# Waits between GpSimd's row gathers in a graph network kernel

## The chip, the cores and the metric

The kernel runs on one core of a Trainium2 chip. The core has five engines that run their own instruction streams and meet only at semaphores: TensorE (PE, matrix products), VectorE (DVE), ScalarE (ACT), GpSimd (POOL) and SyncE (SP, which here only issues transfers). Data is moved between memory (HBM) and the on-chip buffer (SBUF) by 16 DMA engines, on which transfers are queued by SP, ACT or GpSimd. A transfer raises its semaphore by 16 when it has landed. The metric is the device time of one execution in microseconds, the median of three runs.

## The reference

3125 nodes with 256 features each are passed through two layers. Each layer adds to x the output of a graph stage, a mixer, and a mixture of experts. Only the two graph stages gather rows by edge, over 53125 edges sorted by destination:

```python
# layer 0: attention over edges, 4 heads of 64
e = leaky_relu(el[src] + er[dst], 0.2)
ex = exp(e - segment_max(e, dst)[dst])
alpha = ex / segment_sum(ex, dst)[dst]
rst = segment_sum(feat_src[src] * alpha[:, :, None], dst)
# layer 1: weighted sum over edges
support = xn @ weight
agg = segment_sum(support[src] * edge_weight[:, None], dst)
```

The second graph stage is computed as segment_sum(xn[src] * edge_weight) followed by the product with weight, so its gathers fetch rows of 256 numbers.

## The kernel before

The edges are cut into 416 chunks of 128 (NC). A chunk whose destinations cross a border between tiles of 128 nodes is worked on once for each tile, which makes 440 steps (NS). There are 25 tiles of nodes (T).

**The gathers.** One gather is one indirect DMA that GpSimd issues: it fetches 128 rows of a table in HBM, one row to each SBUF partition, at the row numbers that stand in a column of an index tile. `gather_rows` (L483 to L488) fetches rows of `feat_d`, 260 numbers each, into the tile `ring`, which has 24 places (RING) of four steps; step n goes to place n // 4 modulo 24, and the four gathers of a place raise one semaphore, `gathered[place]`. `fetch_rows` (L1205) fetches rows of a table of 256 numbers into the tile `rows`, which has 48 places (RING1) of one chunk, each with a semaphore of its own.

**Where they stand.** The stages run one behind the other, with a barrier of all engines between two. 440 gathers into `ring` are spread over three of them: gathers 0 to 31 in `node_projections`, 32 to 73 in `mixer_and_targets` (L721), and 74 to 439 in `first_aggregate` (L973). In the last, before each fourth gather, GpSimd waits (`once(pool, summed, ...)`) until TensorE has used the place that is to be overwritten, so it can be 96 steps ahead of TensorE at most. 416 gathers into `rows` follow much later: 0 to 19 (PREFILL) in `second_mixer` (L2053), and 20 to 415 in `second_aggregate` (L1264 to L1278). There, before each fourth gather, GpSimd waits until TensorE has finished all but 20 of the steps of that number; it also computes 13 small roots (L1267) in between.

**Who reads them.** In the first aggregation VectorE and ScalarE wait for a whole block of 32 steps before the last four groups of the block ahead, scale the rows (L1086, L1116), and TensorE multiplies them with a one-hot matrix (L1187); VectorE adds the product to its tile (L1071). In the second, TensorE's step n waits for gather n, for VectorE's one-hot matrix (L1286) and for the addition three steps back, multiplies (L1378), and VectorE adds (L1295). Of each 32 steps some also carry a piece of the mixer's attention and of a two-layer network for a pair of tiles (L1385 to L1417).

Nothing in GpSimd's stream waits for a gather to land: the only waits between gathers are those for a free place. The order of the work is written out by hand in each engine's function, without a scheduler.

Of the kernel before, what the change touches and what calls it, by code (L numbers as in the profile page):

```python
# [51 lines left out]
RING = 24  # L52
# [7 lines left out]
AHEAD = 2 * R  # L60
UP_FIRST = 2 * MAXB // UP
RING1 = 48
PREFILL = 20
CLEAR_AT = 18
PARTY = [4, 4, 4, 4, 4, 5]
PARTY_END = [sum(PARTY[:n + 1]) for n in range(len(PARTY))]
assert sum(PARTY) == T
assert NC == CB * SB and NC - RING1 * (NC // RING1) > 0 and RING1 >= T - 1 + 8
assert T % R == 0 and NS == RB * SB and NS % MAXB == 24 and RB <= P
# [67 lines left out]
def once(eng, sem, n, hold=None):  # L137

    if isinstance(n, int) and n <= 0:
        return  # L140
    if hold is None:
        eng.wait_ge(sem, n)
    else:
        hold(eng, sem, n)
# [46 lines left out]
def program(nc, A, out):  # L191
    with ExitStack() as top:
# [69 lines left out]
        with kept:  # L262
# [19 lines left out]
            with Stage(nc) as held:  # L282
                rows = sb("rows", [P, RING1, D], ctx=held)
                step_slot = sb("step_slot", [1, NS], I32, ctx=held)
# [199 lines left out]
def gather_rows(pool, ring, gathered, src_lane, table, n):  # L484

    q, at = divmod(n, 4)
    pool.indirect_dma_start(ring[:, q % RING, at, :], None, table,  # L487
                            bass.IndirectOffsetOnAxis(ap=src_lane[:, n:n + 1], axis=0)).then_inc(gathered[q % RING], 16)  # L488


def node_projections(nc, A, hold, bank, const, big_k, big_v, scores, dst_lane, src_lane, xn_d, xnT_d, feat_d, ring,
                     gathered, end_row, decay, link):

# [192 lines left out]
def mixer_and_targets(nc, A, bank, const, k1, v1, fold, scores, part_er, er, step_tile, src_lane, dst_lo_d, feat_d, ring,  # L686
# [4 lines left out]
    with Stage(nc) as ctx:  # L691
# [27 lines left out]
        @block.gpsimd  # L719
        def _(pool):  # L720
            for n in range(EARLY[NI + 1], BY_THEN):  # L721
                gather_rows(pool, ring, gathered, src_lane, feat_d, n)

        @block.vector
# [140 lines left out]
def first_aggregate(nc, bank, const, acc, er, part_er, dst_lo_d, step_tile, src_lane, dst_lane, feat_d, ring, gathered, masks, decay, link, fold,  # L865
# [10 lines left out]
    with Stage(nc) as ctx:  # L876
# [94 lines left out]
        @block.gpsimd  # L971
        def _(pool):
            for n in range(BY_THEN, NS):  # L973
                if n % Q == 0:
                    once(pool, summed, n - RING * Q + Q)
                gather_rows(pool, ring, gathered, src_lane, feat_d, n)

        @block.vector
# [226 lines left out]
def fetch_rows(pool, rows, gathered, src_of, table, n):  # L1205

    pool.indirect_dma_start(rows[:, n % RING1, :], None, table,  # L1207
                            bass.IndirectOffsetOnAxis(ap=src_of[:, n:n + 1], axis=0)).then_inc(gathered[n % RING1], 16)


def slots_of(nc, eng, step_slot, n, count):

    return nc.values_load_multi_w_load_instructions(
        step_slot[0:1, n:n + count], engines=[eng.engine], min_val=0, max_val=RING1 - 1,
        skip_runtime_bounds_check_because="edge_schedule keeps every slot within the ring")[1]


def second_aggregate(nc, A, bank, const, agg, step_tile, step_slot, src_of, dst_lane, edge_weight, table, rows, gathered, folded,
# [10 lines left out]
    with Stage(nc) as ctx:  # L1229
# [33 lines left out]
        @block.gpsimd  # L1263
        def _(pool):  # L1264
            def root(i):
                pool.wait_ge(found, i + 1)
                pool.tensor_tensor(rstd[:, 0:pair(i)], mv[:, 0:pair(i), 1], const[:, C_POW:C_POW + 1].broadcast_to([P, pair(i)]),  # L1267
                                   ALU.pow).then_inc(rooted, 1)

            for n in range(NC):  # L1270
                i = turn_of(n, ROOT)
                if i is not None:
                    root(i)
                if n < PREFILL:
                    continue
                if n % 4 == 0:
                    once(pool, summed, n + 4 - RING1 + T - 1)
                fetch_rows(pool, rows, gathered, src_of, table, n)  # L1278

        @block.vector  # L1280
# [742 lines left out]
def second_mixer(nc, A, hold, bank, const, big_k, big_v, tops, folded, x2, w_next, w_route, room, src_of, slot_d, step_slot,  # L2023
# [5 lines left out]
    with Stage(nc) as ctx:  # L2029
# [22 lines left out]
        @block.gpsimd  # L2052
        def _(pool):  # L2053
            for n in range(PREFILL):
                fetch_rows(pool, rows, gathered, src_of, table, n)

        @block.vector
# [597 lines left out]
```

## Time and profile before

| | us |
|---|---|
| median of 3 runs | 1989.68 (1985.77 to 1990.58) |
| span of the profiled execution | 2270.7 |
| matmuls of the first aggregation (L1187) | 227.1 to 855.9 |
| matmuls of the second aggregation (L1378) | 1358.0 to 1989.3 |
| GpSimd busy | 1083.0 (48% of the span) |

The profiled execution is one run with the recorder on. Its span is 281 us longer than the median of the runs without it. Busy time counts instructions of an engine, not the time that its DMAs take on the way: for an indirect DMA it is the time in which GpSimd writes the descriptors. Idle time is given with what ended it, as far as the semaphores tell; the name of the releaser can be that of an earlier user of the same semaphore (DMA m_bo<-in_L_mix_bo and DMA m_dst_bc<-dst_lo_d stand for TensorE's `summed` in the two aggregations).

### The profile page before, as it was taken

To read this page: it belongs to the slowest core of one execution; us is meant where nothing else is said; L and a number is where in the kernel's file an instruction comes from. 1 tells how busy PE (TensorE), PEld (TensorE's weight loads), DVE (VectorE), ACT (ScalarE), POOL (GpSimd) and SP (SyncE) were. 2 spreads that over 40 slices of the span, in tenths; PEclk is the share of its full clock that TensorE was granted. 3 is DMA by queue.
4 is the path that set the end of the run, shared out by engine and by line. 5 is a ranking of instruction groups with operands and counts; after the bars stand their busy time and mean duration, and the time that the engine had idled before them with its cause. 6 is when DMAs were issued, how large, how long until landed. Compare 5 with 4: busy or idle time off the path is not lost. (4 is left out here: it accounts for less than half of the span.)

```text
span 2270.7 us, 31260 instructions
## 1 busy us (share of the span) xinstructions
PE 1595.3 (70%) x7757; PEld 1248.9 (55%) x7757; DVE 1257.2 (55%) x3845; ACT 791.0 (35%) x2693; POOL 1083.0 (48%) x1198
## 2 busy tenths in 40 slices
PE   5525566666775876969999756877777877974792
PEld 4523344444444545858888644655555654753692
DVE  3524465655655785736667635555454454676335
ACT  2212454645455674635666430000000000121351
POOL 2562666666666301312112156666566666236441
PEclk9655677777777798979999777887888888986896
DMA  5642444444444206445444223333232233122786
GB/s 183 212 137 63 126 122 124 137 119 127 132 124 121 82 3 226 138 135 164 153 153 153 79 80 107 90 93 87 80 91 84 84 91 92 41 75 82 211 263 216
DMA packets 176878, 276.88 MB, mean 122 GB/s; under 512 B 28920, under 2 KB 132218, under 8 KB 176456
## 3 DMA queue, kind: packets, MB, share of 16 engines
q0 software_dynamic: 50352, 136.58, 20.9%
q1 hardware_dynamic: 82610, 94.62, 13.5%
q10 hardware_dynamic: 43750, 43.75, 5.8%
q8 instruction: 70, 1.15, 0.2%
q14 instruction: 96, 0.79, 0.1%
HBM read 202.35 MB, written 73.58 MB: 122 GB/s over the span
## 5 line engine op out<-in xcount | busy, mean ns | idle before, releaser
L487 POOL DMA_INDIRECT ring<-feat_d,src_lane x440 | 434.4, 987 | 277.5 <-issue 122.3
L1207 POOL DMA_INDIRECT rows<-xn_d,src_of x416 | 404.6, 973 | 244.9 <-issue 115.2
L1187 PE MATMUL bank<-ring,a_hot 128*128 128x260 f32 x880 | 309.6, 503 | 174.9 <-DVE ring L1086 89.3
L1378 PE MATMUL bank<-rows,big 128*128 x880 | 290.0, 445 | 140.4 <-DVE big L1286 79.0
L1187 PEld LDWEIGHTS bank<-ring,a_hot 128*128 128x128 f32 x880 | 205.2, 249 | 245.8 <-DVE ring L1086 107.6
L1116 ACT ACTIVATE ring<-ring 128x64 f32<-128x64 f32 x1320 | 322.7, 336 | 8.1 <-issue 7.3
L1295 DVE TENSOR_TENSOR big<-bank,big 128x256 f32 x440 | 186.7, 424 | 232.1 <-DMA m_bo<-in_L_mix_bo 111.3
L1378 PEld LDWEIGHTS bank<-rows,big 128*128 128x128 f32 x880 | 163.7, 209 | 241.1 <-issue 227.0
L1071 DVE TENSOR_TENSOR acc<-bank,acc 128x260 f32 x440 | 186.5, 424 | 145.7 <-DMA m_dst_bc<-dst_lo_d 72.5
L1348 ACT ACTIVATE big<-bank,a_col 128x256 f32<-128x256 f32 (+1 forms) x26 | 13.0, 552 | 415.1 <-PE bank L1393 263.5
L1286 DVE TENSOR_SCALAR big<-const,dst_lane,ew_lane 128x128 f32<-128x128 f32 x440 | 153.6, 350 | 1.0 <-PEq L93 1.0
L182 POOL TENSOR_TENSOR e_norm_rstd<-e_norm_mv,const 128x1 f32<-128x1 f32 x75 | 42.5, 567 | 230.4 <-DVE e_norm_mv L178 230.4
L182 POOL TENSOR_TENSOR g_norm_rstd<-g_norm_mv,const 128x1 f32<-128x1 f32 x50 | 28.5, 570 | 203.4 <-DVE g_norm_mv L178 203.1
L1976 PE MATMUL bank<-xn1T,top_w 128*128 128x128 f32 x800 | 99.5, 280 | 5.5 <-PEq L93 5.5
L1405 PE MATMUL bank<-big 128*128 128x256 f32 (+1 forms) x416 | 99.6, 384 | 1.8 <-ACT big L1358 1.8
L1976 PEld LDWEIGHTS bank<-xn1T,top_w 128*128 128x128 f32 x800 | 95.9, 196 | 5.9 <-issue 5.6
L1358 ACT ACTIVATE big<-bank,a_b 128x256 f32<-128x256 f32 (+1 forms) x104 | 42.3, 462 | 155.4 <-PE bank L1405 107.1
L1988 PE MATMUL bank<-top_w,e_mid 128*128 128x256 f32 x400 | 94.8, 381 | 0.0
L1417 PE MATMUL bank<-big 128*128 128x256 f32 x400 | 94.5, 379 | 0.0
L1405 PEld LDWEIGHTS bank<-big 128*128 128x128 f32 x416 | 80.1, 198 | 14.4 <-issue 3.0
L2461 POOL DMA_INDIRECT y_d<-e_y,e_to x56 | 54.2, 968 | 68.6 <-DVE e_to L2544 65.5
L1417 PEld LDWEIGHTS bank<-big 128*128 128x128 f32 x400 | 76.0, 190 | 10.3
(399 smaller groups left out, 2912.8 us busy)
## 6 DMA issues: line engine op xcount, KB each, us to landing
slots_d<-fold ACTq DMA_DIRECT2D x25, 1300.0 KB, 5.6
e_w_now<-in_L_ffn_w SPq DMA_DIRECT2D x56, 256.0 KB
a_dst_bc<-dst_lo_d SPq DMA_DIRECT2D x23, 512.0 KB
big<-in_L_ffn_W SPq DMA_DIRECT2D x16, 512.0 KB
e_x<-slots_d SPq DMA_DIRECT2D x56, 130.0 KB
ring<-feat_d,src_lane POOLq DMA_INDIRECT x440
rows<-xn_d,src_of POOLq DMA_INDIRECT x416
e_ys<-y_d SPq DMA_DIRECT2D x24, 256.0 KB
```

Source lines behind the costliest of these rows:

```text
L487: pool.indirect_dma_start(ring[:, q % RING, at, :], None, table, bass.IndirectOffsetOnAxis(ap=src_lane[:, n:n + 1], axis=0)).then_inc(gath ...
L1071: dve.tensor_tensor(to, bank[n % BANKS][:, 0:D + H], to, ALU.add).then_inc(added, 1)
L1116: last = act.activation(part[:, 0:DH], part[:, 0:DH], ACT.Copy, scale=part[:, DH:DW])
L1187: pe.matmul(bank[n % BANKS][:, 0:D + H], hot[:, q % HOTS, at, :], ring[:, q % RING, at, :], start=True, stop=True)\
L1207: pool.indirect_dma_start(rows[:, n % RING1, :], None, table, bass.IndirectOffsetOnAxis(ap=src_of[:, n:n + 1], axis=0)).then_inc(gathered[ ...
L1286: dve.tensor_scalar(hot[:, n % HOTS, :], const[:, C_IOTA:C_IOTA + P], dst_lane[:, n:n + 1], edge_weight[:, n:n + 1], ALU.is_equal, ALU.mul ...
L1295: dve.tensor_tensor(to, bank[n % 4][:, 0:D], to, ALU.add).then_inc(added, 1)
L1378: pe.matmul(bank[n % 4][:, 0:D], hot[:, n % HOTS, :], tile_of(rows, slots[n % 4]), start=True, stop=True)\
L1405: last = pe.matmul(mid_ps[q % 2][:, f * 2 * P:f * 2 * P + m * P], w1[:, k, n * P:(n + 1) * P], lnT[:, k, 0:m * P], start=(k == 0), stop=(k ...
L1417: last = pe.matmul(y_ps[:, t * D:(t + 1) * D], mid[:, f, t * P:(t + 1) * P], w2[:, f, :], start=(f == 0), stop=(f == FT - 1))
L1976: last = pe.matmul(mid_ps[half][:, f * P:(f + 1) * P], w1[:, half, k, f * P:(f + 1) * P], xn1T[:, k, bass.ds(g * P, P)], start=(k == 0), s ...
L1988: last = pe.matmul(y_ps[:, 0:D], mid[:, j, n * P:(n + 1) * P], w2[:, half, f, :], start=(n == 0), stop=(n == FT - 1))
```

## The change

A constant BEHIND = 2 and two helpers are added, with calls in the four places that issue the gathers concerned. `arrived(n - 2)` waits until gather n - 2 into `rows` has landed, before gather n is issued; it stands before each gather of the second set but the first two. `settled(n - 3)` is called before the third gather of each group of four into `ring`, and waits until all four gathers of the group before have landed; gathers 0 to 31 have none. No instruction is moved and none removed.

```diff
+BEHIND = 2
...
+def settled(pool, gathered, n):
+
+    q = n // 4
+    pool.wait_ge(gathered[q % RING], 16 * 4 * (q // RING + 1))
...
             for n in range(EARLY[NI + 1], BY_THEN):
+                if n % 4 == BEHIND:
+                    settled(pool, gathered, n - BEHIND - 1)
                 gather_rows(pool, ring, gathered, src_lane, feat_d, n)
...
             for n in range(BY_THEN, NS):
                 if n % Q == 0:
                     once(pool, summed, n - RING * Q + Q)
+                if n % 4 == BEHIND:
+                    settled(pool, gathered, n - BEHIND - 1)
                 gather_rows(pool, ring, gathered, src_lane, feat_d, n)
...
+def arrived(pool, gathered, n):
+
+    if n >= 0:
+        pool.wait_ge(gathered[n % RING1], n // RING1 * 16 + 16)
...
                 if n % 4 == 0:
                     once(pool, summed, n + 4 - RING1 + T - 1)
+                arrived(pool, gathered, n - BEHIND)
                 fetch_rows(pool, rows, gathered, src_of, table, n)
...
             for n in range(PREFILL):
+                arrived(pool, gathered, n - BEHIND)
                 fetch_rows(pool, rows, gathered, src_of, table, n)
```

GpSimd's stream at the start of the second aggregation, before: gathers of `rows`, and the names in brackets are semaphores that are waited for, under the name of their first user (p1_xnT_stored3 is `summed` here, p1_c_step is `found`).

```order
L1207 DMA rows<-xn_d,src_of 128x256 x4
L1207 DMA rows<-xn_d,src_of 128x256 [waits p1_xnT_stored3]
L1267 TENSOR_TENSOR a_rstd<-a_mv,const 128x2 [waits p1_c_step]
L1207 DMA rows<-xn_d,src_of 128x256 x3
L1207 DMA rows<-xn_d,src_of 128x256 [waits p1_xnT_stored3]
```

The same place now; the lines are 11 and 17 further down, and the other names are the `gathered` semaphores of the places of `rows`.

```order
L1218 DMA rows<-xn_d,src_of 128x256 [waits es_slot_kept]
L1218 DMA rows<-xn_d,src_of 128x256 [waits es_slot_stored]
L1218 DMA rows<-xn_d,src_of 128x256 [waits es_src_in]
L1218 DMA rows<-xn_d,src_of 128x256 [waits es_src_ready]
L1218 DMA rows<-xn_d,src_of 128x256 [waits es_src_turned,p1_xnT_stored3]
L1284 TENSOR_TENSOR a_rstd<-a_mv,const 128x2 [waits p1_c_step]
L1218 DMA rows<-xn_d,src_of 128x256 [waits f_w_in]
L1218 DMA rows<-xn_d,src_of 128x256 [waits f_w_ready]
L1218 DMA rows<-xn_d,src_of 128x256 [waits f_feat_done]
```

Every gather has a wait of its own where one in four had one; their order is the same. In the first aggregation GpSimd's gathers into `ring` now read as follows, where p1_rooted is `summed` and the other names are `gathered` semaphores of groups.

```order
L488 DMA ring<-feat_d,src_lane 128x260 [waits p1_rooted]
L488 DMA ring<-feat_d,src_lane 128x260
L488 DMA ring<-feat_d,src_lane 128x260 [waits f_w_in]
L488 DMA ring<-feat_d,src_lane 128x260
L488 DMA ring<-feat_d,src_lane 128x260 [waits p1_rooted]
```

One gather in four, the third, has the new wait.

## Rows read from the trace of the kernel before

**Rows 1.** the page: span, and GpSimd in 40 slices, busy tenths

```profile
span 2270.7 us, 31260 instructions
...
POOL 2562666666666301312112156666566666236441
```

**Rows 2.** the page's groups: busy, mean ns, idle before and releaser

```profile
L487 POOL DMA_INDIRECT ring<-feat_d,src_lane x440 | 434.4, 987 | 277.5 <-issue 122.3
L1207 POOL DMA_INDIRECT rows<-xn_d,src_of x416 | 404.6, 973 | 244.9 <-issue 115.2
```

**Rows 3.** the gathers of the second aggregation: what they wait for, who waits for them

```profile
L1207 POOL DMA_INDIRECT rows<-xn_d,src_of x416: 940/952/6868, 1309.9 to 1954.7; - x139
...
who waited for it (us, times):
busy tenths in 40 slices 0000000000000000000000056666566666200000
```

**Rows 4.** one tile's instructions, ns min/median/max, first and last start: rows

```profile
L1378 PE MATMUL bank<-rows,big x880: 379/379/791, 1358.0 to 1989.3; 128*128 x176
```

**Rows 5.** the same for the tile ring

```profile
L1187 PE MATMUL bank<-ring,a_hot x880: 382/451/802, 227.1 to 855.9; 128*128 128x260 f32 x176
L487 POOL DMA_INDIRECT ring<-feat_d,src_lane x440: 946/953/1458, 48.4 to 763.3; - x147
```

**Rows 6.** groups by line, GpSimd, 1357 to 1992 us

```profile
L1207 POOL DMA_INDIRECT rows<-xn_d,src_of x396 | 379.5, 958 | 223.4 <-issue 109.4 <-PE bank L1378 62.1 <-DMA m_bo<-in_L_mix_bo 34.7
L1267 POOL TENSOR_TENSOR a_rstd<-a_mv,const 128x2 f32<-128x2 f32 (+1 forms) x13 | 9.6, 739 | 2.3 <-DVE a_mv L1313 2.0
```

**Rows 7.** order of time, GpSimd: start, duration, idle before, the last two gathers

```profile
1953.42 0.95 POOL L1207 DMA_INDIRECT rows<-xn_d,src_of  x1 [0.30 <-issue]
1954.67 0.95 POOL L1207 DMA_INDIRECT rows<-xn_d,src_of  x1 [0.30 <-issue]
```

**Rows 8.** order of time, 27 to 33.5 us: an indirect load and its reader

```profile
28.10 1.01 POOL L365 DMA_INDIRECT es_dst_i<-in_dst,es_chunk  x1 [0.30 <-issue]
...
31.21 0.43 DVE L418 CAST es_rows<-es_dst_i 110x512 f32<-110x512 int32 x1 [11.51 <-issue]
```

**Rows 9.** order of time, 2228 to 2233 us: an indirect store and its waiter

```profile
2230.30 0.97 POOL L2461 DMA_INDIRECT y_d<-e_y,e_to  x1 [0.30 <-issue]
2232.45 0.81 SPq L2451 DMA_DIRECT2D e_ys<-y_d  x2
```

**Rows 10.** short windows behind a last gather; last columns clock, DMA share, GB/s

```profile
176.65:176.90 0.25, 0.00 (x0) 0.00 (x0) 0.00 (x0) 0.00 (x0) 0.00 (x0) 0.50 0.11 33
176.90:177.40 0.50, 0.00 (x0) 0.00 (x0) 0.00 (x0) 0.00 (x0) 0.00 (x0) 0.50 0.00 0
```

**Rows 11.** order of time, 152 to 182 us, the mixer

```profile
152.93 0.42 PE L837 MATMUL bank<-const,acc 128*128 128x128 f32 x1
...
174.43 0.96 POOL L487 DMA_INDIRECT ring<-feat_d,src_lane  x1 [0.31 <-issue]
179.85 0.28 ACT L808 ACTIVATE m_ek<-bank 128x128 f32<-128x128 f32 x1 [26.91 <-DMA ring<-in_x]
```

**Rows 12.** order of time, 1370 to 1388 us, second aggregation

```profile
1370.39 4.51 PE L1378 MATMUL bank<-rows,big 128*128 x14 [0.31 <-DVE big L1286]
...
1378.25 0.42 DVE L1295 TENSOR_TENSOR big<-bank,big 128x256 f32 x1 [2.87 <-DMA m_bo<-in_L_mix_bo]
...
1382.48 0.42 DVE L1295 TENSOR_TENSOR big<-bank,big 128x256 f32 x1 [3.55 <-issue]
...
1387.64 0.94 POOL L1207 DMA_INDIRECT rows<-xn_d,src_of  x1 [3.19 <-DMA m_bo<-in_L_mix_bo]
```

**Rows 13.** line 1378 in two rounds of 32 steps and a piece of the second

```profile
1888.60:1936.80 48.20, 21.33 (x66) 11.94 (x65) 0.85 0.32 90
1936.80:1970.20 33.40, 19.22 (x66) 10.72 (x64) 0.98 0.21 56
1957.20:1970.20 13.00, 12.31 (x41) 6.17 (x41) 1.00 0.02 6
```


## The prediction

> **What bounds the kernel now.** I read the page first, for what GpSimd does and when [rows 1]. The rows to look at are its 40 slices: it is busy for 6 tenths of most slices of the two aggregations, and outside them it has little to do. Nearly all of it is two lines, 440 gathers into ring and 416 into rows [rows 2]. A gather keeps GpSimd for 0.95 us and is followed by 0.30 us of issue, which two neighbours in order of time show: they start at 1953.42 and 1954.67, 1.25 us apart [rows 7]. So a gather costs GpSimd 1.255 us at least, whatever the data does.
>
> Then I asked who waits for the gathers. Nobody does: the view of line 1207 has an empty list under "who waited for it" [rows 3]. What GpSimd itself waits for there, beside issue, is a free place: 62.1 us on TensorE's matmul and 34.7 us under another name of the same semaphore, 97 us in all [rows 6]. In the first aggregation the last gather starts at 763.3 and the last matmul at 855.9, 93 us later [rows 5]; in the second the distance is 1954.7 to 1989.3, 35 us [rows 3, 4]. So in the profiled execution GpSimd runs ahead, and TensorE's steps set the pace: 631 us for 440 steps, from 1358.0 to 1989.3 [rows 4].
>
> But this execution is 281 us longer than the median of the runs, 2270.7 against 1989.68, and I want to know where, because a wait on GpSimd is free only as long as GpSimd has slack. The trace has stretches where a matmul is over by its own record and the reader of its result starts far later. In the mixer, matmul L837 is done at 153.35 and ScalarE, which needs only TensorE's results, starts at 179.85, after 26.9 us of idling, some 4 us behind the last of 42 gathers in a row [rows 11]. In the second aggregation seven steps take 4.51 us, and then VectorE's additions stand at 1378.25 and 1382.48 behind idle times of 2.9 and 3.6 us, and GpSimd at 1387.64 behind 3.2 [rows 12]. The last round of 32 steps, whose second half has no gathers beside it, takes 33.4 us; the round before it, 48.2 us with the same 66 matmul records [rows 13]. Twelve rounds with 13 to 15 us of this each are about 170 us, the mixer's share is 27, and the first aggregation has such holes too. That is the size of the 281 us, so I take it that most of these holes belong to the recorded execution, and that in the timed runs the second aggregation is much shorter than 631 us. How much is a choice: scaled with the whole (1989.68 / 2270.7 = 0.876) it is 553 us; at 33.4 us a round it would need only some 470, and then GpSimd sets the end: 396 gathers x 1.255 = 497, 13 roots of 0.74 us [rows 6] plus issue, some 12, and behind the last gather the landing and 24 steps of 0.65 us (13.0 us for 20 steps, [rows 13]), 19: 528 us. Between 528 and 553 GpSimd has 0 to 25 us of slack over 396 gathers, at most 0.06 us each.
>
> **The change part by part.** Everything hangs on one time, from the end of GpSimd's part of a gather until the gather that waits for it can start; call it x. No row has it, since nothing waits for one of these gathers now. Without the wait, gather n starts 0.30 + 0.95 + 0.30 = 1.55 us behind the end of gather n-2, so up to x = 1.55 the wait is free. With a larger x two gathers take 0.95 + x.
>
> The nearest rows: an indirect store, issued at 2230.30 and 0.97 long, whose waiter on SP issues at 2232.45, gives x = 1.18 [rows 9]. An indirect load, issued at 28.10 and 1.01 long, whose reader on VectorE starts at 31.21, gives x = 2.10 [rows 8]; it is the same direction, HBM to SBUF by row numbers, but of shorter rows. Between them stands what the DMA engines show behind a last gather that ended at 175.39: data starts up to the stretch 176.65 to 176.90 and nothing after it, so the data alone needs 1.3 to 1.5 us, without the semaphore and GpSimd's own start of about 0.3 [rows 10]. That excludes the low row for a gather; I take 2.10. Two gathers then take 3.05 us, one 1.525.
>
> Second aggregation: 396 x 1.525 = 604 us. The 13 roots lie partly in the wait: it has 2.10 - 1.55 = 0.55 us to fill, a root with its issue is 0.93, so 0.4 each, 5 us. Landing and 24 last steps, 19. Sum 628 us. Against 553 that is +75, against 528 it is +100; I take the middle, 540 before, and +88. What is queued behind the waiting gather on GpSimd is only further gathers and the roots; the roots' reader is VectorE (normalise), two steps later in the written order, and TensorE's step n comes to wait for gather n, which is new. The lead of 20 gathers at the start hides the first 20 / (1 - 1.23 / 1.525) or so, about 100 steps; it is used up then, and the sum above, which counts GpSimd's time to the last gather, holds it already. In the profiled execution the same 628 us stand against 631, so its own span should move by -5 to +60 us, the more of the holes stay the more.
>
> The Trainium skill (DMA: Bandwidth & Descriptors, Anatomy of one DMA — SWDGE (gpsimd) path) puts a DMA from GpSimd at about 2.0 us plus its bytes over 436 GB/s. An estimate by that page for 131 KB is 2.30 us from issue to landing, and with 0.30 for GpSimd's start two gathers would take 2.6 us, the second aggregation 396 x 1.30 + 24 = 539 us, the kernel about 1990 to 2000. The row of the load [rows 8] speaks for more.
>
> Prefill in the second mixer: 20 x 1.525 = 31 us instead of 25. In the profile it starts at 1309.9 and holds the one gather of 6.87 us [rows 3], so it is over by 1341, and the next stage's first matmul is at 1358.0 [rows 4]: 17 us of cover where 5.4 are needed, so 0. First aggregation and mixer: the third gather of a group starts 0.30 + 0.95 + 0.30 + 0.95 + 0.30 = 2.80 us behind the end of the last one of the group before, more than 2.10; free. A landing that is late by a microsecond or two costs that once, and the 93 us of lead [rows 5] take it: 0 as forecast, 12 us (one group in six by 0.8 us) as a bound if the lead is gone in the timed runs as well. The wait instructions themselves are 0, they lie inside GpSimd's 0.30 of issue.
>
> Sum: 1989.68 + 88 = 2078 us.
>
> **The rivals.** (1) The landing is hidden: x is 1.6 or less in the timed runs, since no packet is recorded there. For it: the store's 1.18 and the data's 1.3 to 1.5 [rows 9, 10]. Against: the load's 2.10. Time: 1990 at x = 1.55, and up to 2010 at 1.65 (0.05 us each on 396). (2) The other side: the holes are real. They stand only where gathers follow each other without a pause [rows 11 to 13], and a slower rate of gathers ends them. It decides if a pace between 1.255 and about 1.40 us is enough: then the gathers still fit into the 553 us stage, and TensorE gets back part of its holes. One hole of about 2 us in each of 12 rounds is 24 us: 1966. Against it: a stage cannot be shorter than its gathers, 628 us at x = 2.10, and the mixer's 42 gathers with the longest hole would not be slowed at all. (3) GpSimd has more slack than I take, because the timed stage is nearer to 600: then +28 to +40, 2025. (4) The wait doesn't bind because the semaphore of n-2 is long raised: that is rival 1.
>
> **How the numbers follow.** GpSimd sets the end of the second aggregation: 0.62, between 2038 and 2105 (x from 1.90 to 2.20 makes +48 to +108 against 540, and some us of the first aggregation's bound come on top); forecast 2078. Rival 3: 0.10. Rival 1 with no change: 0.13; with a small loss up to 2010: 0.05. Rival 2: 0.10. A measurement of this kernel can tell about 0.3% from no change, 6 us. Faster 0.10, within it 0.13, slower 0.77. The range reaches from 1984, which takes in no change, to 2105, and leaves out rival 2 and landings above 2.20 us.
>
> **What would show it.** In the profile after, gathers of rows should start about 1.5 us apart on average instead of 1.26, GpSimd's idle time in the second aggregation should be named by the gathers' own semaphores, and TensorE's step should now wait for a gather. Gathers into ring should keep their 1.26 us. If starts in the second aggregation stay 1.25 us apart in pairs, x was below 1.55 and I am wrong by the whole 88 us. If the rounds of 32 steps shrink toward 34 us while gathers go on, rival 2 is right. If the gathers are 1.5 us apart and the timed runs don't move, the slack that I took away from GpSimd was there.

## The result, and the profile after

The change makes the kernel slower: 2161.7 us, median of 4 runs (2160.9 to 2163.9), against 1988.6 for the kernel before beside it (1985.8 to 1990.6). The ratio is 1.0877, interval 1.0861 to 1.0893, so +173 us. I had forecast +88 us, 2078, with a range up to 2105. The direction was right, the size and the range were not.

The profiled execution of the kernel after has a span of 2162.2 us, the same as its timed runs. The first recording of the kernel before had 281 us more than its timed runs, so it is a poor partner. The kernel before was recorded once more (the run e14_before_again, below): span 1981.9. All comparisons of traces from here on use that recording.

The page of the kernel after: the span, GpSimd in 40 slices, and the groups that answer to [rows 1, 2], with busy time, mean ns and the idle time before.

```profile
span 2162.2 us, 31358 instructions
...
POOL 3677777777772132121114556555556555247341
...
L1218 POOL DMA_INDIRECT rows<-xn_d,src_of x416 | 403.9, 971 | 301.1 <-DMA rows<-xn_d,src_of 215.6
L488 POOL DMA_INDIRECT ring<-feat_d,src_lane x440 | 441.2, 1003 | 176.1 <-issue 116.7
L1396 PE MATMUL bank<-rows,big 128*128 x880 | 363.8, 521 | 136.5 <-DMA rows<-xn_d,src_of 113.1
```

GpSimd is busy for 5 tenths of a slice in the second aggregation; the idle time before its gathers is now put down to the gathers themselves, 215.6 us of it, where [rows 2] had issue. And TensorE waits for gathers, 113.1 us. What GpSimd waits for in the second aggregation, in total us, times and longest, in the kernel after:

```profile
POOL rows L1218 <- DMA rows<-xn_d,src_of: 203.2, 259, 3.4
POOL rows L1218 <- PE bank L1396: 35.3, 34, 1.9
```

and in the second recording of the kernel before:

```profile
POOL rows L1208 <- issue: 109.5, 364, 0.3
POOL rows L1208 <- PE bank L1379: 9.7, 29, 1.2
```

and what TensorE waits for there, in that second recording:

```profile
PE bank L1379 <- DMA rows<-xn_d,src_of: 29.7, 43, 1.7
```

Already before the change TensorE waits for gathers, 43 times, where [rows 3] showed nobody waiting; and GpSimd waits 9.7 us for a free place, not the 97 us of [rows 6]. GpSimd was the bound. The empty list of [rows 3] was no evidence: the first recording holds no landing of any gather, so nobody could be seen to wait for one. Its list of DMA issues gives the gathers no time to landing,

```profile
rows<-xn_d,src_of POOLq DMA_INDIRECT x416
```

where the second recording has a median of 2.8 us, from the part of the gathers (166 of the 396) whose landing it holds:

```profile
rows<-xn_d,src_of POOLq DMA_INDIRECT x416, 2.8
```

First and last starts (us, after the durations in ns), as in [rows 3 to 5]. The kernel before, second recording, the tile ring:

```profile
L1188 PE MATMUL bank<-ring,a_hot x880: 382/383/802, 170.6 to 684.4; 128*128 128x260 f32 x176
L488 POOL DMA_INDIRECT ring<-feat_d,src_lane x440: 946/953/1455, 43.9 to 640.9; - x147
```

and the tile rows:

```profile
L1379 PE MATMUL bank<-rows,big x880: 379/379/791, 1171.7 to 1702.4; 128*128 x176
L1208 POOL DMA_INDIRECT rows<-xn_d,src_of x416: 942/952/7287, 1138.8 to 1679.0; - x139
```

The kernel after, ring:

```profile
L1198 PE MATMUL bank<-ring,a_hot x880: 382/383/802, 172.2 to 707.1; 128*128 128x260 f32 x176
L488 POOL DMA_INDIRECT ring<-feat_d,src_lane x440: 949/957/1458, 43.4 to 663.5; - x147
```

and rows:

```profile
L1396 PE MATMUL bank<-rows,big x880: 379/478/791, 1198.1 to 1884.2; 128*128 x176
L1218 POOL DMA_INDIRECT rows<-xn_d,src_of x416: 943/955/6172, 1158.5 to 1858.0; - x139
DMA to landing us min/median/max: 2.7/2.8/4.0
```

The second aggregation takes 686.1 us instead of 530.7, +155. It also begins 26.4 us later, and 22.7 of those are there already at the end of the first aggregation (707.1 against 684.4). Behind it nothing changes much (278.0 against 279.5 us to the end). So two places to explain: +155, where I had +88, and +23, where I had 0.

GpSimd in order of time in the kernel after (start, duration, in brackets idle before):

```profile
1501.54 0.95 POOL L1218 DMA_INDIRECT rows<-xn_d,src_of  x1 [0.30 <-issue]
1503.34 0.95 POOL L1218 DMA_INDIRECT rows<-xn_d,src_of  x1 [0.85 <-DMA rows<-xn_d,src_of]
1504.59 0.94 POOL L1218 DMA_INDIRECT rows<-xn_d,src_of  x1 [0.31 <-DMA rows<-xn_d,src_of]
1506.37 0.95 POOL L1218 DMA_INDIRECT rows<-xn_d,src_of  x1 [0.84 <-DMA rows<-xn_d,src_of]
1508.07 0.95 POOL L1218 DMA_INDIRECT rows<-xn_d,src_of  x1 [0.75 <-DMA rows<-xn_d,src_of]
```

and the instruction at line 1225 (the wait in `arrived`) between 1504.3 and 1509.4 us:

```profile
L1225 POOLq EVENT_SEMAPHORE  x1: 17/17/17, 1507.4 to 1507.4; - x1
```

A gather starts 3.03 to 3.05 us after the one before the last (1501.54 to 1504.59, 1503.34 to 1506.37). That is x = 2.08 to 2.10 behind the end of a gather of 0.95, what I had taken. But the gather at 1508.07 starts 3.48 us after the one at 1504.59, and it is the one with the separate instruction. Every fourth gather has two waits, for gather n-2 and for TensorE's count of steps; the gather carries the one that is written first, the other becomes an instruction of its own, 98 of them in the whole trace. It was over at 1507.4, and the gather began 0.7 us later. Counted from the landing that is waited for, where the trace has it, such a gather starts 0.74 us behind it and one with a single late wait 0.26, so the pair costs 0.48 us at its place. Over the whole stage (differences of the start times, from gather 20 on, by n mod 4) such a gather starts 2.12 us after its neighbour, the others 1.39, 1.76 and 1.41; the mean is 1.67 where my sum had 1.525. The traces of the changed kernels hold the landings of about half of the gathers (here 199 of the 396), so every figure on landings below is that of a sample.

### The profile page after: what moved, and what is told of

Read it like the earlier page. It is cut to its first block and busy times, and to the rows that moved or that the text cites. A ratio compares the mean times of both kernels' runs of the same rounds, so it can differ in the third digit from the quotient of the medians.

```text
span 2162.2 us, 31358 instructions
## 1 busy us (share of the span) xinstructions
PE 1620.0 (75%) x7757; PEld 1238.2 (57%) x7757; DVE 1261.6 (58%) x3845; ACT 791.2 (37%) x2693; POOL 1089.5 (50%) x1198
## 5 line engine op out<-in xcount | busy, mean ns | idle before, releaser
L1218 POOL DMA_INDIRECT rows<-xn_d,src_of x416 | 403.9, 971 | 301.1 <-DMA rows<-xn_d,src_of 215.6
L488 POOL DMA_INDIRECT ring<-feat_d,src_lane x440 | 441.2, 1003 | 176.1 <-issue 116.7
L1396 PE MATMUL bank<-rows,big 128*128 x880 | 363.8, 521 | 136.5 <-DMA rows<-xn_d,src_of 113.1
L1396 PEld LDWEIGHTS bank<-rows,big 128*128 128x128 f32 x880 | 180.7, 238 | 294.2 <-issue 284.7
L1198 PE MATMUL bank<-ring,a_hot 128*128 128x260 f32 x880 | 266.8, 453 | 42.6 <-DVE ring L1097 36.9
L1198 PEld LDWEIGHTS bank<-ring,a_hot 128*128 128x128 f32 x880 | 185.4, 223 | 96.0 <-DVE ring L1097 48.4
```

The source lines that it names most:

```text
L1198: pe.matmul(bank[n % BANKS][:, 0:D + H], hot[:, q % HOTS, at, :], ring[:, q % RING, at, :], start=True, stop=True)\
L1396: pe.matmul(bank[n % 4][:, 0:D], hot[:, n % HOTS, :], tile_of(rows, slots[n % 4]), start=True, stop=True)\
```

## The experiments

All medians are in us; the ratio is to the kernel before on the same chip, whose median lay between 1982 and 1989 from one set of runs to the next, so differences of a few us between runs of different sets mean nothing. "Spacing" is the mean difference of the start times of the gathers into rows from gather 20 on, read in order of time. The kernel before has 1.285, the changed one 1.671.

**One part alone: the second aggregation.** `settled` is not called, and neither is `arrived` in the 20 first fills; `arrived` stays in the second aggregation.

```diff
-                if n % 4 == BEHIND:
-                    settled(pool, gathered, n - BEHIND - 1)
```

> Only the 396 gathers of the second aggregation wait for gather n-2; the waits of the first set, of the mixer and of the 20 prefilled gathers are gone. Theory: the whole loss lies in the second aggregation, where GpSimd's gathers set the pace, so this is as slow as the changed kernel, +173 us on before (+168 to +178). Rival: the waits of the first set cost part of it; then this is at least 12 us faster than the changed kernel.

2137.9 (2131.7 to 2146.7), ratio 1.0763 [1.0718, 1.0809]: +153. The spacing is 1.670 as in the changed kernel. I had expected +168 to +178, the whole loss; it is 24 us less, so the rival is right and the first set costs part.

**The other part alone: the first set.** `arrived` is not called; `settled` stays.

```diff
-                arrived(pool, gathered, n - BEHIND)
```

> Only the third gather of each group of the first set waits. Theory: its own semaphore comes 0.7 us before GpSimd could start anyway, so the time is that of before, within 6 us. Rival: late landings cost it 12 us or more. The recorded execution tells besides whether the holes of TensorE in the first set's stages go away with this wait (span well under 2270 us) or stay.

2009.8 (2005.1 to 2013.1), ratio 1.0122 [1.0093, 1.0152]: +25, where I had expected no more than 6; the rival, 12 us or more by late landings, is right. The two parts add up, 153 + 25 = 178 against 173. What GpSimd waits for between 172 and 665 us, the kernel before having no row of a DMA there:

```profile
POOL ring L488 <- issue: 96.3, 316, 0.3
POOL ring L488 <- DMA ring<-feat_d,src_lane: 27.6, 20, 3.3
```

In that stage 92 groups have the wait. Twenty of them find a gather of the group before not landed, 27.6 us in all, and the first aggregation's last matmul moves by 20.6 us, from 684.4 to 705.0. This recording has the second aggregation without any pacing again at 531 us (its matmuls go from 1196.6 to 1727.7).

**One gather more under way.** `BEHIND = 3` instead of 2, so a gather waits for n-3, and in the first set the fourth gather of a group waits for the group before.

```diff
-BEHIND = 2
+BEHIND = 3
```

> Gather n waits for gather n-3, and the fourth gather of a group for the group before. Theory (latency chain): a gather needs 2.76 us to land and GpSimd 0.26 us to start, 3.02 us in all, and three gathers take 3.77 us by themselves, so the wait is free but for the fourth gather of four, which has two waits: at most 0.47 us each on 99 gathers. 0 to +46 us on before. Rival (any wait on GpSimd costs its own time): 0.4 us on each of 396 gathers remains, +150 us.

2000.9 (1994.5 to 2003.0), ratio 1.0073 [1.0050, 1.0096]: +14, where the whole change costs 173, so a wait does not cost its own time on every gather and that rival is out. The spacing is 1.31. In the first set two waits of 20 are left:

```profile
POOL ring L488 <- DMA ring<-feat_d,src_lane: 1.1, 2, 0.8
```

**Fewer gathers with two waits.** The changed kernel, with TensorE's count waited for ahead of every sixteenth gather, each wait for a count that covers the next sixteen.

```diff
-                if n % 4 == 0:
-                    once(pool, summed, n + 4 - RING1 + T - 1)
+                if n % 16 == 4 and n >= 36:
+                    once(pool, summed, n + 16 - RING1 + T - 1)
```

> The changed kernel, but the wait for a free place stands before every sixteenth gather of the second aggregation and not before every fourth. In the changed kernel's trace a gather with both waits starts 1.07 us behind the last data packet of gather n-2, one with a single wait 0.6 us. Theory (a second wait costs about 0.47 us of start): 74 of 99 double waits gone make the kernel 30 to 38 us faster than the changed one. Rival (the gather simply waits for its place, or for a late landing): within 6 us of the changed kernel.

2136.4 (2128.1 to 2139.0), ratio 1.0751 [1.0716, 1.0787]: 25 us less than the changed kernel. The spacing falls to 1.60; the 24 gathers that still have two waits start 1.90 us after their neighbour, all others, in the mean by place among 16, between 1.40 and 1.73. So the second wait is a cost of its own. The pairs that are gone make 25 us in the time and 395 x (1.671 - 1.598) = 29 us in the gathers. I had expected 30 to 38; 29 us for some 74 pairs is 0.4 each and not the 0.48 that a pair takes at its place.

**The same waits in the other order.** The changed kernel, with two calls exchanged.

```diff
+                arrived(pool, gathered, n - BEHIND)
                 if n % 4 == 0:
                     once(pool, summed, n + 4 - RING1 + T - 1)
-                arrived(pool, gathered, n - BEHIND)
```

> The changed kernel with the two waits of every fourth gather in the second aggregation in the other order: first the landing of gather n-2, then the count of TensorE's steps. Theory (the wait that stands first in the code becomes an instruction's own wait or a separate instruction, and what costs 0.45 us is that the one which really ends late is the separate one): the late one now sits on the gather itself or on the nearer place, the spacing before every fourth gather falls from 2.11 to about 1.65, the mean from 1.67 to about 1.56, and the kernel takes 2115 to 2140. Rival (two waits cost 0.45 us in any order once one of them ends late): 2155 to 2165, spacing 2.1 as before.

2130.0 (2125.6 to 2133.4), ratio 1.0737 [1.0713, 1.0761]: 32 us less than the changed kernel by the medians, 28 by the two ratios (1.0877 and 1.0737), for an exchange of two lines. The separate instruction is now `once` (line 143), as often as before:

```profile
L143 POOLq EVENT_SEMAPHORE  x98: 17/17/17, 1212.6 to 1818.9; - x98
```

GpSimd in order of time; the gather at 1507.08 is one with two waits:

```profile
1504.02 1.00 POOL L1218 DMA_INDIRECT rows<-xn_d,src_of  x1 [0.79 <-DMA rows<-xn_d,src_of]
1505.32 0.95 POOL L1218 DMA_INDIRECT rows<-xn_d,src_of  x1 [0.30 <-DMA rows<-xn_d,src_of]
1507.08 0.95 POOL L1218 DMA_INDIRECT rows<-xn_d,src_of  x1 [0.80 <-DMA rows<-xn_d,src_of]
1508.33 0.95 POOL L1218 DMA_INDIRECT rows<-xn_d,src_of  x1 [0.30 <-DMA rows<-xn_d,src_of]
```

It starts 3.06 us after the gather at 1504.02, like its neighbours: the wait that ends late is on the gather, the separate one had long been met. The spacing is 1.571, and 395 x (1.671 - 1.571) = 40 us, which is 0.4 us for each of the 98 pairs. Some 30 of the 40 show in the time: in this recording the second aggregation begins 7.5 us later than in the changed kernel's (1205.6 and 1198.1), and late landings in the first aggregation took 33.2 us of GpSimd's time in all instead of 24.6.

**Waits that are always met.** The kernel before with `arrived(pool, gathered, n - 8)` ahead of each gather of the second aggregation and none in the first set.

```diff
-                arrived(pool, gathered, n - BEHIND)
+                arrived(pool, gathered, n - 8)
```

> The kernel before with a wait ahead of every gather of the second aggregation, on gather n-8 instead of n-2, and none in the first set: the same number of wait instructions as the change puts there, all on something that landed over 7 us ago. Theory (a satisfied wait is covered by the 0.30 us between two gathers): at most +4, 1983 to 1991. Rival (each wait costs GpSimd some hundredths of a microsecond, or a gather with two of them some tenths): +10 to +40, 1995 to 2025.

1983.7 against 1982.8, ratio 0.9999 [0.9985, 1.0012]. Its trace has the same 98 separate instructions as the changed kernel, and a spacing of 1.285, that of the kernel before:

```profile
L1221 POOLq EVENT_SEMAPHORE  x98: 17/17/17, 1174.0 to 1668.5; - x98
```

So neither a wait nor a pair of them costs anything while both are met. The 0.48 us is paid only where the separate instruction is the one that ends late. That is when it is paid; why it is paid, no run shows.

**One gather at a time.** The second aggregation alone is paced, each gather waits for n-1, with the order of the waits exchanged as above.

```diff
-                arrived(pool, gathered, n - BEHIND)
+                arrived(pool, gathered, n - 1)
```

> The kernel with waits in the second aggregation alone, each gather waiting for the one just before it, the count of TensorE's steps waited for second. Theory (what GpSimd pays between two waited-for gathers is the landing, 2.76 us after the start, and 0.26 us to go on): the spacing is 2.76 + 0.26 = 3.02 us, 396 of them 1196 us instead of 509, plus what landing late adds at a few; the kernel takes 1983 + 687 = 2670, range 2660 to 2700. Rival (with one gather under way instead of two the landing itself is shorter, since two gathers share the DMA engines): spacing 2.7 or less, 2540 or less.

2727.9 (2724.0 to 2729.7), ratio 1.3748 [1.3718, 1.3779]: +742, outside my 2660 to 2700. In order of time:

```profile
1500.34 0.96 POOL L1214 DMA_INDIRECT rows<-xn_d,src_of  x1 [2.08 <-DMA rows<-xn_d,src_of]
1503.36 0.96 POOL L1214 DMA_INDIRECT rows<-xn_d,src_of  x1 [2.07 <-DMA rows<-xn_d,src_of]
1506.44 0.96 POOL L1214 DMA_INDIRECT rows<-xn_d,src_of  x1 [2.12 <-DMA rows<-xn_d,src_of]
```

The starts are 3.02 us apart in the middle, as expected, and the median landing is 2.76 us where it is 2.77 with two under way, so a landing is not made shorter by having no other gather beside it: the rival is out. The mean is 3.08, because one in sixteen is more than 3.4; that is 23 us. The rest I had left out: the 20 first fills, in the second mixer, take 3 us each too, outlast that stage, and the second aggregation begins at 1206.0 instead of 1171.7, 34 us.

**Half rows.** The kernel of the exchanged waits, with rows of 512 B. TensorE reads the half row twice.

```diff
-    pool.indirect_dma_start(rows[:, n % RING1, :], None, table,
+    pool.indirect_dma_start(rows[:, n % RING1, 0:P], None, table.rearrange("n (a b) -> (n a) b", b=P),
```

> The kernel with both sets of waits and the second aggregation's pair of waits swapped (2130 us, spacing 1.571), in which each gather of the second aggregation, the first fills of its ring too, fetches rows of 512 B instead of 1 KB: half of each row is left out and the other half used twice, so the output is another. Theory (the landing is nearly all fixed time, since 128 KB in it makes few packets for each of the 16 engines): the median landing stays at 2.7 to 2.76 us after the start, the spacing at 1.53 to 1.57, the kernel takes 2112 to 2132. Rival, by the DMA queue's time being bytes over a rate on top of 2.0 us (the Trainium skill, DMA: Bandwidth & Descriptors, Anatomy of one DMA): 0.15 us less per landing, so 0.075 less per gather, 396 of them 30 us, 2100.

2085.7 (2079.6 to 2088.2), ratio 1.0521 [1.0496, 1.0546]: 44 us less than with whole rows, so my theory of a fixed time fell. The line on landings:

```profile
DMA to landing us min/median/max: 2.4/2.5/3.8
```

It reads 2.7/2.8 for whole rows. Unrounded the medians in the trace are 2.54 and 2.77: 64 KB less per gather is 0.23 us less. The spacing goes from 1.571 to 1.473, and 395 x 0.098 = 39 us of the 44. If the landing goes up evenly with the bytes, which two sizes can't show, 0.23 us for 64 KB leave some 2.3 us that bytes do not change, GpSimd's own 0.95 among them. The Trainium skill (DMA: Bandwidth & Descriptors, Anatomy of one DMA — SWDGE (gpsimd) path) has 2.0 us plus bytes over 436 GB/s: an estimate by it is 0.15 us for the 64 KB, and 2.30 for the whole where the trace has 2.77. The trace agrees that fewer bytes land earlier and that most of the time does not depend on them; by size the rule is low on both terms here.

**Small loads.** The kernel with waits in the first set alone, with SP's broadcasts (dst_bc) cut from 512 KB to 64 KB.

```diff
-                sp.dma_start(dst_bc[:, w % 2, 0:n, :],
+                few = 1024 if w < 2 else 128
+                sp.dma_start(dst_bc[:, w % 2, 0:n, 0:few],
```

> The kernel with waits in the first set of gathers alone (25 us slower than before), with SP's broadcasts of destinations in the first aggregation cut from 512 KB to 64 KB each, all but the first two (the destinations of most look-ups are stale, so the output is another). Theory (the 20 or so gathers that land 3.5 to 5.4 us after they began are late because they share the 16 DMA engines with those broadcasts, and the wait for the group before turns each late landing into a hole of about 1 us): the landings' 95% point falls from 4.5 to below 3.3 us, third gathers that start over 1.6 us after the one before fall from 18 to at most 5, and the kernel takes 1985 to 1993. Rival (the late landings come from something else, the row loads and stores of the mixer among them): still 15 or more such gathers, 2005 to 2012.

1992.6 (1988.6 to 1994.9), ratio 1.0042 [1.0023, 1.0061]: of the +25 us, +8 are left, inside the 1985 to 1993 that I had expected.

```profile
POOL ring L488 <- DMA ring<-feat_d,src_lane: 9.8, 14, 1.6
```

The waits fall from 27.6 us to 9.8, the slowest twentieth of the landings that the traces hold from over 4.5 us to over 3.9; I had expected 3.3. Third gathers that start over 1.6 us behind the one before fall from 24 (the expectation has 18) to 12, not to 5. So those broadcasts make two thirds of the time that is waited, and half of the long waits. What makes the others was not tried; the row loads and stores of the same stage are candidates.

**Lighter TensorE.** The kernel before with some of the small network's matmuls left out.

```diff
-                    for k in range(KT):
+                    for k in range(1):
...
-                for f in range(4 * half, 4 * half + 4):
+                for f in range(4 * half, 4 * half + 1):
```

> The kernel before with TensorE's work in the second aggregation made lighter: the first layer of the small network multiplies only the first half of its inputs (half of its matmuls left out) and the second layer only one of each four hidden tiles (three quarters left out), so the output is another. Some 50 us of the 95 and some 70 us of the 95 that those two groups are busy go. Theory (GpSimd's 396 gathers at 1.26 us set the second aggregation): its TensorE work still takes about 528 us and the kernel stays within 10 us of before, 1975 to 1987. Rival (TensorE's own 520-odd us of matmuls in that stage are as much the bound as the gathers): the stage loses 30 us or more, 1955 or less.

1977.6 against 1982.8, ratio 0.9972 [0.9957, 0.9986]: 5 us for leaving out over 100 us of matmuls, and the spacing stays at 1.284. TensorE's busy time in the stage falls by less than what was left out, from 485.0 to 441.4 us, because the granted clock is 0.80 there instead of 0.90; even so it idles for 86 us of 528. TensorE was not what the second aggregation waited for.

**Fills on GpSimd.** The kernel before with 50 fills of 128x2 between its gathers.

```diff
+                if n % 8 == 6:
+                    pool.memset(idle[:, n // 8 * 2:n // 8 * 2 + 2], 0.0)
```

> The kernel before with 50 small fills of 128x2 added on GpSimd, one ahead of every eighth gather of the second aggregation, into places that nobody reads: the disputed question is how much GpSimd can be late there before the kernel is. Theory (no slack, GpSimd's queue sets the stage): each costs what one lasts with its start, 0.3 to 1.0 us, and all of it reaches the end: with the duration d read from its rows, 50 x d, between +15 and +50 in the kernel, the spacing of gathers rising by the same. Rival (TensorE has 20 or more us of slack to GpSimd): less than a third of the sum that the rows of the fills give reaches the end.

1981.9 against 1982.8, ratio 1.0007 [0.9995, 1.0019]. This told nothing, and the rows say why:

```profile
1507.01 0.95 POOL L1207 DMA_INDIRECT rows<-xn_d,src_of  x1 [0.30 <-issue]
1507.95 0.11 POOL L1280 MEMSET a_idle<- 128x2 f32 x1
1508.26 0.95 POOL L1207 DMA_INDIRECT rows<-xn_d,src_of  x1 [0.19 <-issue]
```

The fill of 0.11 us and the 0.19 behind it make the same 0.30 us that stand between two gathers without it; the gathers are 1.25 us apart as before. My sum, 50 times its duration, was wrong.

**Powers on GpSimd.** The same with something longer than the gap.

```diff
+                if n % 8 == 6:
+                    pool.tensor_tensor(idle[:, n // 8 * 2:n // 8 * 2 + 2], const[:, C_ONE:C_ONE + 2],
+                                       const[:, C_POW:C_POW + 1].broadcast_to([P, 2]), ALU.pow)
```

> The kernel before with 50 powers of 128x2 added on GpSimd, one ahead of every eighth gather of the second aggregation, into places that nobody reads. The fills of the run before lasted 0.13 us and were gone in the 0.30 us between two gathers, so they tested nothing; the kernel's own such powers last 0.7 us and put the next gather 1.98 us after the one before instead of 1.257. Theory (GpSimd's queue sets the stage and it has no slack): 50 x 0.72 = +36, between +28 and +40 in the kernel, 2010 to 2024, the mean spacing of gathers 1.285 to about 1.375. Rival (TensorE's own work, busy 520 of 531 us there, hides most of it): less than +12.

2014.9 (2013.9 to 2018.7), ratio 1.0163 [1.0140, 1.0187]: +29 to 32 us. The groups of the stage:

```profile
L1280 POOL TENSOR_TENSOR a_idle<-const 128x2 f32<-128x2 f32 x50 | 37.9, 757 | 1.1
L1268 POOL TENSOR_TENSOR a_rstd<-a_mv,const 128x2 f32<-128x2 f32 (+1 forms) x13 | 9.4, 724 | 0.3
```

37.9 us of added work, some 30 of them at the end of the kernel, with a spacing of 1.372: GpSimd has next to no slack.

**The kernel before, and one with a shorter GpSimd queue.** In the second, ScalarE takes the 13 square roots and VectorE their reciprocals, so that GpSimd only gathers.

```diff
-                pool.tensor_tensor(rstd[:, 0:pair(i)], mv[:, 0:pair(i), 1], const[:, C_POW:C_POW + 1].broadcast_to([P, pair(i)]),
-                                   ALU.pow).then_inc(rooted, 1)
...
+                act.activation(mv[:, 0:pair(i), 1], mv[:, 0:pair(i), 1], ACT.Sqrt).then_inc(square, 1)
...
+                dve.reciprocal(rstd[:, 0:pair(i)], mv[:, 0:pair(i), 1]).then_inc(rooted, 1)
```

> The kernel before, unchanged, recorded once more. Theory (the holes of its first recording are not the kernel's): a span of 1980 to 1995 us, the second aggregation's matmuls from about 1170 to 1702, 531 us, gathers 1.285 us apart. Rival (this program is one that holes appear in whenever it is recorded): a span above 2100.

> The kernel before with the 13 inverse square roots of the second aggregation taken from GpSimd: ScalarE takes the square root of the same two columns and VectorE its reciprocal. Theory (GpSimd's queue alone sets the stage): each root put 0.72 us between two gathers, 13 of them 9.4 us; all but the one or two behind the last gather go, so -7 to -9 us, 1974 to 1979, the mean spacing of gathers 1.285 to about 1.262. Rival (TensorE's 520 us of matmuls are next in line at once, or ScalarE's changes of function cost its chain time): within 3 us of before, or slower.

The kernel before, recorded again, has a span of 1981.9 and no holes. The one without roots on GpSimd takes 1974.2 (1970.1 to 1977.3), ratio 0.9954 [0.9938, 0.9971]: 8 us faster than before, little but clear of the noise, its spacing 1.257, its matmuls over rows in 522.1 us instead of 530.7:

```profile
L1379 PE MATMUL bank<-rows,big x880: 379/379/792, 1172.2 to 1694.3; 128*128 x176
```

and ScalarE's groups in the same stretch:

```profile
L1339 ACT ACT_TABLE_LOAD x13 | 16.7, 1283 | 6.8 <-PEq L93 6.6
L1358 ACT ACT_TABLE_LOAD x13 | 16.7, 1283 | 61.8 <-PE bank L1406 61.8
```

The table loads that the square root brings cost ScalarE 33 us, in time in which it waits anyway. This version is the fastest of the three. A longer queue on GpSimd lengthens the stage, a shorter one shortens it by as much: the queue is the bound.

## Why the prediction was wrong

**The holes belong to the recorded execution: right.** Second recording 1981.9 us, against timed runs of 1979 to 1993; every other kernel's recording fits its timed runs as well. What made the holes in the first one is open. That GpSimd sets the end of the stage was right as well (e5, e9, e13), so rival 3, more slack, is out. I took 540 us for the second aggregation before, between 528 by GpSimd's sum and 553 by scaling. It is 530.7. The sum from GpSimd's rows was right within 3 us; moving halfway to a scaled number cost 9.

**x = 2.10: the value was right, the row it came from was not; that was luck.** 2.07 to 2.12 in the rows of e11 and of the changed kernel; the hidden landing (rival 1) and the store of [rows 9] are out. But the same load and reader as in [rows 8] stand in the second recording as

```profile
27.96 1.01 POOL L366 DMA_INDIRECT es_dst_i<-in_dst,es_chunk  x1 [0.30 <-issue]
30.72 0.43 DVE L419 CAST es_rows<-es_dst_i 110x512 f32<-110x512 int32 x1 [11.88 <-DMA es_dst_i<-in_dst,es_chunk]
```

which gives x = 1.75, and in the other fourteen recordings the pair gives from 1.60 to 3.38. With 1.75 my sum would have been 396 x 1.35 + 24 = 559 us, +19 and not +88. One row of another transfer, taken from one recording, could not carry this number; of the gathers themselves, a second recording of the kernel before would have given the landing (median 2.77 us from the start, 1.82 from the end of GpSimd's part), with only GpSimd's 0.26 us of starting unknown.

**"The wait instructions themselves are 0": the step that failed.** It holds for waits that are met (e7: 98 separate ones, no time) and for one wait that ends late. It does not hold for a gather with two waits of which the separate one ends late. Every fourth gather was one: it starts 0.74 us behind the landing instead of 0.26, and the stage pays 0.4 us net for each of the 98. The exchange of two lines takes some 30 us off the time and brings the stage from 686.1 to 646.9 us. It is the largest term of the miss and not all of it: the kernel with the exchange, 2130, lies above my range too. Reading the code would have shown the pair, `once` and `arrived` on the same gather; the trace of before had no wait for a landing, so no row could give the price, and I should have bounded it.

**396 x 1.525 = 604, 628 with its ends: mis-sized by 19 us besides.** With the waits exchanged the stage takes 646.9. Two parts make it. The last gather starts at 1826.2 and the last matmul at 1852.5, 26 us for the landing and the last steps where I had 19: 7 us. And the spacing is 1.571 where 1.525 and the roots make 1.54: 0.03 a gather, some 12 us. Most of that are landings later than the median: one in twenty comes more than 3.1 us after its start, the mean is 2.81 against a median of 2.77, and half of the 0.04 is 0.02 a gather or 9 us. I had the median in the sum and not the mean. The rest of the 12 us is not traced; GpSimd's 12.4 us of waits for a free place in that recording may be it. The rule of the Trainium skill that I set beside it (DMA: Bandwidth & Descriptors, Anatomy of one DMA — SWDGE (gpsimd) path; 2.30 us, kernel at 1990 to 2000) was further off.

**"The 93 us of lead take it": failed.** In the second recording the distance from the last gather into ring to the last matmul is 43.5 us (640.9 to 684.4), and it is 43.6 in the changed kernel (663.5 to 707.1). It is no lead at all, since it doesn't shrink when the gathers are late: the other 50 us of the 93 were there only in the recording with the holes. GpSimd was the bound in this stage as well: in the second recording its waits for a free place there are 0.3 us at most, 7.9 us in all. So the 20-odd us of late landings came through in full, +23 (e2: +25). My bound, 12 us, assumed one group in six late by 0.8; it is one in five (19 of 92), and each waits 1.3 us (24.6 us in the changed kernel between 172 and 665 us):

```profile
POOL ring L488 <- DMA ring<-feat_d,src_lane: 24.6, 19, 2.2
```

**Prefill 0: right.** Of the 26.4 us by which the second aggregation begins late, 22.7 come from the first. The other 3.7 are not the fills' waits: e2, which has none there, takes 491.6 us from the last matmul of the first aggregation to the first of the second, the changed kernel 491.0, the second recording of before 487.3.

**The sum again.** 88 forecast, + 9 for the stage before, + 39 for the double waits (686.1 - 646.9), + 19 for the rest of the paced stage, + 23 for the first set: 178. The spans of the two recordings differ by 180, the timed runs by 173. TensorE's clock moved as well. The second aggregation in the kernel after (busy us and count of PE, PEld, DVE, ACT, POOL, then the granted clock, DMA share, GB/s):

```profile
1198.10:1884.20 686.10, 559.69 (x1845) 371.99 (x1846) 339.02 (x1002) 57.14 (x131) 388.71 (x409) 0.77 0.28 79
```

and in the second recording of before:

```profile
1171.70:1702.40 530.70, 485.03 (x1845) 346.45 (x1846) 332.33 (x1002) 57.14 (x131) 388.58 (x409) 0.90 0.36 103
```

TensorE, with longer gaps before its matmuls now, is granted 0.77 of 2.4 GHz instead of 0.90, a longer share of the stretch at 1.2 GHz, and the same 1845 matmuls last 560 us instead of 485. It is still idle for 126 of 686 us, and GpSimd sets the pace, so I count nothing for it in the sum; that is argued, no run separated it. Rival 2, a gain from ended holes, had nothing to gain, since the timed runs are as short as the recording without holes.

## What to carry to other kernels

When a wait for a landing is added to an instruction that has a wait already, write it so that the one that ends late is the instruction's own (in this kernel, the one written first), and look in the trace for the separate one; here the order of two lines was worth some 30 us. A pacing wait sets the distance between transfers to the landing and restart (here 3.02 us) divided by how many may be under way, and it costs what that exceeds the engine's own distance (here 1.26): 1.51 for two under way, where the kernel loses 7% even with the waits in the better order, and 1.01 for three, where it loses 0.7%, the first set's waits included both times. And where a recorded span is far above the timed runs, take slack neither from it nor from a scaled copy of it: sum the busiest queue's own rows, or record the kernel again. Before an empty list of waiters is read as slack, look whether the recording holds the landings at all.

## What the runs showed of the hardware

- A gather of 128 rows of 1 KB lands 2.77 us after GpSimd starts it (median), one of 512 B rows 2.54; GpSimd starts the waiting one 0.26 us after the landing (3.02 between starts less 2.76 in e11).
- Where a gather has two waits and the separate one ends last, the gather starts 0.74 us behind the landing instead of 0.26 (the changed kernel against e6).
- Between two gathers lie 0.30 us. A fill of 0.11 us costs nothing there, since the next gather starts 0.19 us behind it (e8). Of a power of 0.76 us most is paid: 50 of them, 37.9 us, cost some 30 (e9).
- Beside broadcasts of 512 KB one gather in twenty lands more than 4.5 us after its start; with 64 KB ones it is 3.9 (e2, e10).
